# Where three turns, a projection and a batch's final sums stand in the order of a fused attention and expert kernel

## The reference, cut to what matters

```python
# 1. window attention, windows of 8x8 pixels, 4 heads of 16 channels, residual
n = (x - mean_c(x)) / sqrt(var_c(x) + 1e-6)            # over the 64 channels of a pixel
q, k, v = split_heads(n @ Wq + bq, n @ Wkv + bkv)
p = softmax(q @ k.T / 4 + bias)                        # 64x64 for each window and head
x = x + (p @ v) @ Wproj + bproj
# 2. two of eight experts for each token (pixel), residual
t = tokens(x);  m = (t - mean(t)) / sqrt(var(t) + 1e-5)
r = softmax(m @ router_w + router_b);  top, idx = top_k(r, 2);  top = top / sum(top)
t = t + sum_k top[k] * (m @ expert_w[idx[k]] + expert_b[idx[k]])
```

## Time and profile before

| what | value |
|---|---|
| median of three runs | 1537.11 us (1533.65 to 1537.75) |
| the profiled execution | 1533.56 us |
| its span, first to last instruction | 1531.7 us |
| TensorE: matmuls busy / weight loads busy | 1333.5 us (87%) / 824.9 us (54%) |
| VectorE busy | 1195.6 us (78%) |
| ScalarE busy | 884.2 us (58%) |
| GpSimd busy | 886.8 us (58%) |
| mean granted TensorE clock | 0.984 of full |

### The profile page before, as it was taken

The page is one execution under the profiler, slowest core; times in us unless marked ns, Lnnn a source line. Parts: engine busy times, 40 slices in busy tenths (PEclk is TensorE's granted clock), DMA queues, the critical chain, the costliest instruction groups (busy, mean ns, idle before and its releaser), DMA issues.

```text
span 1531.7 us, 49805 instructions
## 1 busy us (share of the span) xinstructions
PE 1333.5 (87%) x18247; PEld 824.9 (54%) x18432; DVE 1195.6 (78%) x2486; ACT 884.2 (58%) x1672; POOL 886.8 (58%) x731
## 2 busy tenths in 40 slices
PE   4488999988898999988898899998989999999976
PEld 3255555555555555555555555555555555555541
DVE  7548888977776888987787688898778777787764
ACT  5356666646555666655555566664655566565631
POOL 0246555668654655658856455566875656656532
PEclk9999999999999999999999999999999999999998
DMA  6012333222122233222122233322212222122221
GB/s 169 1 31 57 73 77 76 60 51 55 41 50 53 71 77 77 57 70 53 39 58 50 57 81 77 72 64 51 59 38 54 53 58 55 38 56 50 58 58 35
DMA packets 95212, 90.23 MB, mean 59 GB/s; under 512 B 26653, under 2 KB 62045, under 8 KB 95070
## 3 DMA queue, kind: packets, MB, share of 16 engines
q1 hardware_dynamic: 95070, 88.30, 24.5%
HBM read 35.83 MB, written 17.83 MB: 35 GB/s over the span
## 4 chain that ended last, share of the span: by engine, by line
DVE 33%; PE 25%; POOL 16%; issue 16%; ACT 3%; DMA 3%; DVEq 1%; SPq 1%; POOLq 1%; another core or an unknown queue 1%; ACTq 0%
PE bank_g L502 7%; DVE t_g L954 5%; PE bank_p L375 5%; PE bank_y L513 5%; POOL ln L1050 4%; DVE mx L849 3%; DVE x L871 3%; DVE sums L798 3%; DVE sums L790 3%; POOL prob L1038 2%; DVE prob L842 2%; POOL rstd L1022 2%; PE bank_e L473 2%; POOL t_g L1060 2%; DVE bank_e L883 2%
## 5 line engine op out<-in xcount | busy, mean ns | idle before, releaser
L954 DVE TENSOR_TENSOR t_g<-t_t,bank_g 128x512 f32<-128x512 f32 x384 | 262.9, 685 | 164.3 <-PE bank_g L502 153.7
L513 PE MATMUL bank_y<-t_g,w_exp 128*64 128x512 f32 x1024 | 272.5, 611 | 30.4 <-issue 15.6
L653 ACT ACTIVATE prob<-prob 128x512 f32<-128x512 f32 x256 | 159.9, 626 | 202.7 <-POOL prob L1038 202.6
L1038 POOL TENSOR_TENSOR prob<-prob,mx 128x512 f32<-128x512 f32 x256 | 262.0, 1046 | 2.5 <-DVE mx L849 2.5
L1060 POOL TENSOR_TENSOR t_g<-t_t,g_copy 128x512 f32<-128x512 f32 x128 | 164.8, 1288 | 169.5 <-ACT g_copy L685 166.5
L375 PE MATMUL bank_p<-xn,w_qkv 128*64 128x256 f32 x1536 | 215.2, 400 | 33.2 <-POOL xn L1032 17.7
L1029 POOL TENSOR_TENSOR xn<-xt,rstd 128x512 f32 (+1 forms) x64 | 81.7, 1277 | 240.4 <-PE bank_p L375 238.3
L842 DVE TENSOR_TENSOR prob<-bank_s,rel 128x1024 f32<-128x1024 f32 x128 | 156.4, 1222 | 72.1 <-PE bank_s L401 64.5
L657 ACT ACTIVATE prob_t<-bank_t 128x512 f32<-128x512 f32 x256 | 152.3, 595 | 66.2 <-PE bank_t L416 66.2
L1050 POOL TENSOR_TENSOR ln<-ln,mhalf 128x8 f32<-128x8 f32 x64 | 104.8, 1637 | 145.8 <-DVE ln L885 145.8
L502 PE MATMUL bank_g<-g_t,gate_sel 128*128 128x512 bf16 x390 | 151.7, 389 | 42.9 <-DVE t_g L954 41.3
(11 more groups left out here) (108 smaller groups left out, 2359.4 us busy)
## 6 DMA issues: line engine op xcount, KB each, us to landing
t_t<-t_rout SPq DMA_DIRECT2D x256, 128.0 KB, 3.7
x_in<-in_x SPq DMA_DIRECT2D x68, 256.0 KB, 3.2
r_b<-recip_rows SPq DMA_DIRECT2D x64, 256.0 KB
out_y<-y_out SPq DMA_DIRECT2D x128, 128.0 KB, 2.3
r_in<-sum_b SPq DMA_DIRECT2D x64, 16.0 KB
recip_rows<-r_out SPq DMA_DIRECT2D x64, 16.0 KB, 1.4
rel<-in_relb SPq DMA_DIRECT2D x1, 256.0 KB
gate_sel<-in_sel SPq DMA_DIRECT2D x1, 256.0 KB
```

Source lines behind the costliest of these rows:

```text
L513: mm(B_Y[C * a:C * a + C, :], w_exp[:, pair, :], t_g[:, (2 * pair + a) % TG, :], start=False, stop=(pair == MIXES // 2 - 1), skip_group_ch ...
L653: A(prob[:, i], prob[:, i], ACT.Exp).then_inc(p_ready.sem, 1)
L954: V.tensor_tensor(t_g[:, u % TG, :], t_t[:, p, u % 2, :], B_G[:, :], ALU.mult).then_inc(tg_dve.sem, 1)
L1038: G.tensor_tensor(sc, sc, mx[:, i, :].unsqueeze(2).broadcast_to([P, 2 * HEADS, NTOK]), ALU.subtract).then_inc(s_shifted.sem, 1)
```

## The change

In TensorE's and ScalarE's order, the second turn of probabilities (and its copy) goes ahead of the tokens' turn (and its copy) in slots without `take`; the q projection and its copy go ahead, and the logits go behind the q projection and behind `gates(2)`. `statistics` is cut in two, and both parts move from the end of the `sums`-only slot to two places near the start of the next slot, which is the first `power` slot.

```diff
@@ pipeline
-                slot(b * STRIPS + 11, 1, Work(b + 1, sums=(3, 1), up=True), on)
+                slot(b * STRIPS + 11, 1, Work(b + 1, sums=(3, 1)), on)
                 for n in range(RSTD_PARTS // 2):
-                    slot(b * STRIPS + (12 + n), n % 2, Work(b + 1, power=2 * n), on)
+                    slot(b * STRIPS + (12 + n), n % 2, Work(b + 1, up=n == 0, power=2 * n), on)
@@ slot of TensorE
                 if mixing:
                     start_sum(j - 3, 1 - p)
                     gates(j - 3, 0)
+                if attending and not work.take:
+                    turn_probs(j, 1, work)
                 if routing_on:
                     turn_tokens(j - 2)
                 if work.take:
                     take(work.batch, *work.take, 0, j)
-                if attending and not work.take:
+                if mixing:
+                    gates(j - 3, 1)
+                if projecting:
+                    project(j + 1, 0)
+                if attending and work.take:
                     turn_probs(j, 1, work)
                 if mixing:
-                    gates(j - 3, 1)
+                    gates(j - 3, 2)
                 if routing_on:
                     logits(j - 2)
-                if attending and work.take:
-                    turn_probs(j, 1, work)
-                if mixing:
-                    gates(j - 3, 2)
-                if projecting:
-                    project(j + 1, 0)
                 if mixing:
                     experts(j - 3, 0)
                     gates(j - 3, 3)
@@ slot of ScalarE
+                if attending and not work.take:
+                    copy_probs(j, 1)
                 if routing_on:
                     copy_tokens(j - 2)
                 if work.take:
                     take(work.batch, *work.take, 0, B_T[:, :])
-                if attending:
-                    copy_probs(j, 1)
-                    exps(j, 2)
-                if mixing:
-                    copy_gates(j - 3, 2)
-                if attending:
-                    exps(j, 3)
                 if projecting:
                     copy_q(j + 1, 1 - p)
+                if attending and work.take:
+                    copy_probs(j, 1)
+                if attending:
+                    exps(j, 2)
+                if mixing:
+                    copy_gates(j - 3, 2)
+                if attending:
+                    exps(j, 3)
@@ slot of VectorE (total_sums = L809, L810; variances = L812 to L819)
                 if work.sums:
                     sum_planes(work.batch, *work.sums)
+                if work.up:
+                    total_sums(work.batch)
                 if mixing:
                     gate(j - 3, 1 - p, 0)
                 if outputting:
                     reciprocals(j - 1)
                 if work.sums:
                     sum_squares(work.batch, *work.sums)
+                if work.up:
+                    variances(work.batch)
                 if mixing:
                     gate(j - 3, 1 - p, 1)
...
                 if mixing:
                     gate(j - 3, 1 - p, 7)
-                if work.up:
-                    statistics(work.batch)
```

More of the change, by code:

```diff
@@ L537, in slot @@
                     take(work.batch, *work.take, 0, j)
-                if attending and not work.take:
-                    turn_probs(j, 1, work)
                 if mixing:
                     gates(j - 3, 1)
-                if routing_on:
-                    logits(j - 2)
+                if projecting:
+                    project(j + 1, 0)
                 if attending and work.take:
@@ L547, in slot @@
                     gates(j - 3, 2)
-                if projecting:
-                    project(j + 1, 0)
+                if routing_on:
+                    logits(j - 2)
                 if mixing:
@@ L710, in slot @@
                     take(work.batch, *work.take, 0, B_T[:, :])
+                if projecting:
+                    copy_q(j + 1, 1 - p)
+                if attending and work.take:
+                    copy_probs(j, 1)
                 if attending:
-                    copy_probs(j, 1)
                     exps(j, 2)
@@ L717, in slot @@
                     exps(j, 3)
-                if projecting:
-                    copy_q(j + 1, 1 - p)
                 if attending:
@@ L804, in first_sums, with total_sums @@
                 sum_squares(batch, t, r)
-            def statistics(batch):
+            def total_sums(batch):
                 dve.wait_ge(part_sums.sem, part_sums.at(batch * GROUPS + GROUPS))
@@ L810, in statistics, with variances @@
                 V.tensor_reduce(st[:, 1, :], sums2[:, :, :], AX.X, ALU.add).then_inc(stat.sem, 1)
+            def variances(batch):
                 dve.wait_ge(stat.sem, stat.at(batch, 2))
@@ L835, in first_statistics @@
             def first_statistics(batch):
-                statistics(batch)
+                total_sums(batch)
+                variances(batch)
                 first_deviations()
```

## The result

| | before | after |
|---|---|---|
| median | 1537.01 us (1533.65 to 1537.75, 4 runs) | 1565.48 us (1559.47 to 1566.21, 4 runs) |
| ratio | | 1.0181 [1.0152, 1.021] |
| profiled execution / its span | 1533.56 / 1531.7 us | 1565.12 / 1563.3 us |
| mean granted TensorE clock | 0.984 | 0.982 |

The change costs 28.5 us. The forecast was +43 (1580 us): the sign and the mechanism came true, the size was too large by half.

The account below looks back on a forecast made before the run. VectorE's order was taken to bound 24 slots, with both branches ending together in plain ones. +29.5 (slots with sums), +3.6 (`take` alone), +16.1 (plain), -6.0 (statistics) make +43.2: 1580 us, range 1568 to 1590, wider 1564 to 1593.

Parts of the forecast that it names:

- the wait that would grow: VectorE's wait for the logits over the whole span, forecast to go from 22.8 to about 90 us.
- Part 2: The 24 plain slots: logits behind the q projection and `gates(2)` delay gate 3 by 0.67 us each, +16.1 us.
- The `take` slots with sums: With the sums-only slots, 24 slots: VectorE stands behind gate 1 for the logits, gate 3 +1.23 us each, +29.5 us.
- The slots with `take` alone: Three slots without sums, given the value of the nearest slots, 1.2 us each, +3.6 us.
- a real gain for TensorE: Plain slots: the turn of probabilities, about half a microsecond, fits into TensorE's wait between `gates(0)` and the tokens.
- ScalarE and the order of the q copy at 0: The earlier q copy pushes `exps(2)`, the gate 2 copy and `exps(3)` back some 0.8 us, at a cost of 0.
- that cover: GpSimd's later gate 2 feeds experts behind a later gate 3; without this cover, 0.8 us in each of 60 slots.
- The statistics: Moving them saves 3 x 3.61 us in sums-only slots and costs 3 x 1.6 in first `power` slots: -6.0 us.
- Fill and drain at 0: The slots at both ends, where there is no projection or no mixing, were taken to change by 0 us.
- A: Rival: TensorE binds and the change fills its waits, so the kernel gets faster, 1514 us; chance 0.05.
- B: Rival: only VectorE-bound and `take` slots pay, plain slots hide theirs, statistics cost nothing: +22, 1559 us; chance 0.11.
- C: Rival: nothing is taken up, plain slots lose 1.06 us each, `power` slots their whole shift: +59, 1597 us; chance 0.08.

Follow-up runs that it names:

- experiment 7: Kernel after with only `gates(2)` and the logits swapped, the logits staying behind the q projection: 1534.29 us.
- experiment 4: Kernel before with only the second turn of probabilities and its copy ahead of the tokens' turn in slots without `take`: 1539.80 us.
- experiment 6: Kernel after with only ScalarE's q copy put back behind `exps(3)`: 1562.54 us.
- experiment 1: Kernel after with only the logits taken back right behind `gates(1)`, ahead of the q projection: 1567.15 us.
- experiment 5: Kernel after with the logits right behind `gates(1)` and ScalarE's q copy back behind `exps(3)`: 1543.61 us.
- experiment 2: Kernel before with only the logits moved behind `gates(2)`, still ahead of the q projection: 1592.09 us.
- experiment 3: Kernel before with only the statistics cut and moved to the two places in the next slot: 1532.65 us.
- experiment 9: Kernel before with the statistics moved and the q projection ahead of `gates(2)` only in slots with sums, logits still first: 1520.97 us.

## Why the prediction came out right in kind and too high in size

**What bounds the kernel: right.** It named the place (VectorE standing behind gate 1 for a full trip through TensorE), the wait that would grow and to what total. Experiment 7 shows the cause in the 24 slots with sums: of the 28 us that swapping `gates(2)` and the logits gives back in the full slots, 24 lie there. In the plain slots most of the loss has another cause, the q projection ahead of the logits: only 0.12 of 0.43 us comes back with the swap. Part 2 of the forecast has that cost. The total of the wait was forecast well, though the single wait in a `take` slot was 1.28 us and not 1.5.

**The `take` slots with sums: right mechanism, 1.23 us forecast, 0.89 measured.** The terms of the sum that failed were two hand-overs. (a) "The next group starts 0.32 us later" and "the logits take 1.07": behind `gates(2)` they are 591.65 - 591.43 = 0.22 and 0.96, so L909 is 1.22 us behind `gates(2)` where I had 1.42. I took both from groups that had another kind of group ahead of them. (b) L902 to gate 3 was read as 2.43 us from a plain slot of before and called free of waits. After, it is 2.27 us (592.65 to 594.92) in the means of all kinds of slot but the first `power` slot (2.63). In that plain slot of before, the last routing step was

```profile
1320.50 0.23 DVE L922 TENSOR_TENSOR bank_e<-bank_e,rs 128x64 f32<-128x64 f32 x1
```

and gate 3 started 0.32 us behind its start (1320.82); in the plain slot of after it is 0.17 (1344.24 to 1344.41). Gate 3 started 0.04 us behind the end of `gates(3)`, out at 1320.78 by my own reading, so it was most likely held by it for 0.16 us. A row without a bracket is not proof that nothing was waited for. Less 0.20 and 0.16, the 1.23 become 0.87, which is what the slot shows. In 21 slots that is 7 us of the 11.6 by which the sum (43.2) missed the difference of the spans (31.6). The slots with `take` alone were put at 1.2 and gave 0.96, 0.81 in the pair that ran at full clock (22.15 and 22.96 us).

**The plain slots: 0.67 forecast, 0.43 measured, 6 us too much.** The same two terms, and one that made up for a part. In the slot shown `gates(2)` came 0.12 us later than I had it (4.85 us behind the slot's start, not 4.73), the way from it to L909 was 0.19 shorter, so L909 came +0.67 where I had +0.74; and with the shorter way to gate 3, gate 3 came only +0.50. The sentence that the turn of the probabilities is "a real gain for TensorE" was half true: the wait for tokens halves, but experiment 4 finds it again as a wait for the tokens' copy.

**ScalarE and the order of the q copy at 0: right for this kernel, and for a narrower reason than given.** The text asked what it would cost "if that cover were gone" and put 0.8 us in 60 slots, but looked for the cover in GpSimd's gate 2. The cover is the late routing: experiment 6 shows 0 under it, experiments 1 and 5 show 23.5 us without it (16 of them in the 60 full slots, 0.27 us a slot), through the gate bank: `gates(3)` overwrites what ScalarE copies for GpSimd, and the prediction did not count that wait.

**The statistics: near.** The sums-only slot was forecast at -2.4 and is -2.63 in the mean; the three differ (-4.3, -2.7, -0.85), and part of that is the clock (before 0.87, 1.00 and 0.93; after 1.00, 1.00 and 0.86), so the mean is not clean. The one pair at full clock on both sides gives -2.73. The first power slot was forecast at +1.6 and is +1.34; the others 0, as forecast.

**Fill and drain at 0: not shown to be wrong.** Fill and drain differ (-2.6 and +5.2 us), but with the clock. Stretches of the kernel after, with the columns of experiment 2: a sums-only slot and the drain.

```profile
1047.84:1072.50 24.66, 22.89 (x285) 13.60 (x285) 19.95 (x40) 12.61 (x25) 12.78 (x11) 0.86 0.20 44
...
1526.51:1563.00 36.49, 23.94 (x74) 7.86 (x72) 12.62 (x32) 5.07 (x10) 7.82 (x6) 0.69 0.13 29
```

The same stretch of the kernel before:

```profile
1497.64:1531.00 33.36, 21.13 (x73) 6.41 (x72) 12.61 (x32) 5.19 (x10) 7.77 (x6) 0.85 0.14 32
```

VectorE, ScalarE and GpSimd do the same in both; TensorE was granted less of its clock, 0.69 against 0.85, and the stretch is 3.1 us longer. That the order does this isn't shown. From the third last start of L1050 to the end it is 72.3 us before and 77.5 after; but in experiments 3 and 9, which leave the drain in before's order, it is 77.9 and 76.2. The slot of fill took 20.3 us at a clock of 0.83 before and 17.6 at 1.00 after; in experiment 9, with before's order there, it took 17.9 at 1.00. The 60 full slots alone differ by 27.8 us, close to the 28.5 of the medians.

**The rivals.** A needed TensorE to bind and falls by experiments 4 and 7. B (+22) had the plain slots at nothing and C (+59) took nothing up; both failed on the plain slots, which paid 0.43. That the total lies between B and the forecast is no point for B's mechanism. Every part of the sum came out too high, so the nearness of the total owes nothing to errors that cancelled. That the wide range still held the median, by 1.5 us, is partly luck: one of the four runs (1559.47 us) lies outside it.

## What to carry to other kernels

On engines that work in order, look for the round trip: X ends a step, Y may go on only then, and X's next instruction wants what Y makes after that. Let Y make first what X wants next, and put into Y's wait something that X doesn't want; here the wrong order of two neighbours cost some 30 us, and the right filling with the moved sums brought 1.0% against the kernel before. Where two branches end together, undoing one edit of several can show nothing or a loss, since the other branch then decides: change both, or swap the two neighbours in dispute and nothing else.

## What the runs showed of the hardware

- The granted clock can fall behind small waits. In experiment 2 the mean is 0.967, and single slots stand at 0.87 with groups of 1.98 and 1.92 us for 1.08. What TensorE did before that fall were the waits of 0.71 and 0.78 us shown there. Yet the kernel after has waits of 0.59 us (the `take` slot shown) and of 1.28 us (ahead of `gates(4)` in the plain slot shown) in slots at a clock of 1.00, so such a wait alone isn't enough; what decides it stays open. The Trainium skill ("TensorE: Matmul & The Clock Gate", section "A second HAM failure mode: psum-queue depth-cycling") tells of a kernel in which short idle times between groups of matmuls, while it goes round PSUM banks, made the clock swing. Here too the waits that came before the fall stand between groups of matmuls; that the cause is the same no run here shows.
- Runs of one kernel spread with the clock, though not strictly in its order: four executions of the kernel after took 1559.47, 1565.12, 1565.84 and 1566.21 us at 0.986, 0.982, 0.980 and 0.976. Differences of 3 to 5 us, as in experiments 3 and 4, were not clear of that with ten runs. Slots at the same place of the loop mostly repeat to 0.05 us where the clock is 1.00 (22.88, 22.88 and 22.87 us for one of the `take` slots of before), so a comparison slot by slot shows what the medians hide.
- The same eight matmuls of the logits last 0.96 us behind `gates(2)` in the kernel after and behind the turned probabilities in experiment 7, and 1.07 in the old place. Behind the start of `gates(2)` the logits begin after 0.22 us and the q projection after 0.32. Why stays open.
